# Dealing the rows of tiles 4 to 63 to gather units of falling width, with sums added onto the output

## What is computed

```python
h = jnp.maximum(_layernorm(x, axis=-1), 0.0)
hw = (h @ W.T).reshape(n, 8, 32)
attn = einsum(hw, a_src)[:, None, :] + einsum(hw, a_dst)[None, :, :] + adj[:, :, None] * We[:, 0] + be
attn = jnp.where((adj > 0)[:, :, None], attn, -jnp.inf)
attn = softmax(leaky_relu(attn, 0.2), axis=1)
out = x + einsum('ijh,jhd->ihd', attn, hw).reshape(n, 256) + h @ Wr.T + br
```

## Time and profile before

| | us |
|---|---|
| median of 3 runs | 2900.41 |
| profiled execution, whole time | 2904.47 |
| its span, first to last instruction | 2902.8 |
| front, to the first MAX8 | 0 to 217 |
| gather stage | 217 to 2590 |
| dense stage | 2590 to 2903 |
| VectorE busy | 2346.5 (81%) |
| GpSimd busy | 1844.2 (64%) |
| ScalarE busy | 1625.0 (56%) |
| TensorE busy | 1587.1 (55%) |

### The profile page before, as it was taken

How to read it: one execution, slowest core, us unless ns; L and a number is a source line. 1 busy time by engine, 2 the same in 40 slices (tenths; PEclk the granted TensorE clock), 3 DMA queues, 4 the chain that set the end, 5 groups by cost and what they waited for, 6 DMA issues and landing times.

```text
span 2902.8 us, 31846 instructions
## 1 busy us (share of the span) xinstructions
PE 1587.1 (55%) x5859; PEld 1067.1 (37%) x5860; DVE 2346.5 (81%) x5737; ACT 1625.0 (56%) x6849; POOL 1844.2 (64%) x1914
## 2 busy tenths in 40 slices
PE   6980044332353554456565667566565656445886
PEld 4650043322242433233333334333333433324665
DVE  3449676676786878799999999999999999929993
ACT  2220022222354665577777878777777867565663
POOL 3654777777777777777777777777777776510000
PEclk9995576666675666666666656566666656667998
DMA  3454634444545555566666677767667666437670
GB/s 97 144 187 139 187 93 113 120 124 142 153 134 158 162 166 167 163 176 200 195 196 202 202 212 211 217 196 221 202 214 211 198 210 208 126 130 171 186 175 2
DMA packets 254494, 486.91 MB, mean 168 GB/s; under 512 B 119232, under 2 KB 150464, under 8 KB 252144
## 3 DMA queue, kind: packets, MB, share of 16 engines
q1 hardware_dynamic: 151280, 319.60, 36.1%
q0 software_dynamic: 84752, 148.94, 19.5%
q10 hardware_dynamic: 18288, 16.65, 1.8%
HBM read 549.09 MB, written 25.76 MB: 198 GB/s over the span
## 4 chain that ended last, share of the span: by engine, by line
issue 31%; DMA 27%; POOL 18%; DVE 11%; PE 8%; ACT 2%; POOLq 1%; SPq 0%; DVEq 0%; ACTq 0%; PEldq 0%
DMA gath<-table,offs 25%; POOL gath L413 18%; DVE work L509 3%; DVE work L505 3%; PE banks L933 2%; PE banks L927 2%; ACT gath L795 2%; DMA adj_sb<-in_adj_dram 1%; PE banks L930 1%; PE banks L1014 1%; PE banks L1004 1%; PE banks L956 1%; DVE adj_sb L681 1%; DVE gath L620 0%; POOLq L413 0%
## 5 line engine op out<-in xcount | busy, mean ns | idle before, releaser
L413 POOL DMA_INDIRECT gath<-table,offs x1637 | 1711.7, 1046 | 611.5 <-issue 411.7
L795 ACT ACTIVATE gath<-gath,prob 128x32 f32<-128x32 f32 x6416 | 1366.4, 307 | 110.5 <-DVE prob L608 110.5
L956 PE MATMUL banks<-gath,ident 128*128 128x256 f32 x1670 | 511.6, 479 | 892.5 <-DVE gath L620 892.5
L963 PE MATMUL banks<-gath,ident 128*128 128x256 f32 x1604 | 631.8, 514 | 281.4 <-ACT gath L795 281.1
L956 PEld LDWEIGHTS banks<-gath,ident 128*128 128x128 f32 x1670 | 407.8, 249 | 1013.2 <-DVE gath L620 935.7
L509 DVE FIND_INDEX8 work<-work,adj_sb 128x8 uint32<-128x176 f32 (+30 forms) x833 | 645.5, 798 | 0.7 <-issue 0.6
L505 DVE MAX8 work<-adj_sb 128x8 f32<-128x176 f32 (+30 forms) x833 | 593.4, 789 | 9.9 <-DMA adj_sb<-in_adj_dram 9.9
L963 PEld LDWEIGHTS banks<-gath,ident 128*128 128x128 f32 x1604 | 329.1, 235 | 556.8 <-ACT gath L795 537.8
L790 ACT ACTIVATE prob<-pre 128x176 f32<-128x176 f32 (+23 forms) x63 | 23.7, 376 | 850.5 <-DVE pre L598 849.6
L620 DVE TENSOR_TENSOR gath<-gath,prob 128x1024 f32<-128x1024 f32 (+8 forms) x171 | 240.2, 1457 | 2.1 <-issue 0.2
L587 DVE TENSOR_TENSOR pre<-pre,gath 128x136 f32<-128x136 f32 (+23 forms) x80 | 24.2, 320 | 263.5 <-DMA gath<-table,offs 258.0
(11 more groups left out here) (110 smaller groups left out, 1589.4 us busy)
## 6 DMA issues: line engine op xcount, KB each, us to landing
adj_sb<-in_adj_dram SPq DMA_DIRECT2D x504, 512.0 KB, 3.7
gath<-dst_rows SPq DMA_DIRECT2D x16, 2048.0 KB, 8.8
gath<-table,offs POOLq DMA_INDIRECT x1637
table<-gath POOLq DMA_DIRECT2D x32, 264.0 KB, 2.9
gath<-in_x_dram SPq DMA_DIRECT2D x32, 256.0 KB, 3.0
resid<-gath POOLq DMA_DIRECT2D x32, 256.0 KB, 2.6
work<-table SPq DMA_DIRECT2D x8, 1024.0 KB, 10.8
res_sb<-resid ACTq DMA_DIRECT2D x63, 128.0 KB
```

The costliest lines, as they stand in the source:

```text
L413: pool.indirect_dma_start(gath[:, ph.slot(b, k), :], None, table[:, :], bass.IndirectOffsetOnAxis(ap=offs[:, b, k:k + 1], axis=0), bounds_ ...
L795: last = s.activation(g, g, ACT.Copy, scale=prob[:, k * H + h:k * H + h + 1])
L956: last = m.matmul(ps_sum[:, b, :], ident[:, :], gath[:, ph.slot(b, k), 0:HD], start=False, stop=False)
L963: last = m.matmul(ps_sum[:, b, :], ident[:, :], gath[:, ph.slot(b, k), 0:HD], start=False, stop=(k == K - 1))
```

## The change

- Tiles 1 to 3 stay as they are ("direct"). Tiles 4 to 63 form groups of 4, 8, 8, 8, 8, 8, 8 and 8 tiles. Within a group all rows are ordered by falling edge count, and the first 128 go to the first unit, the next 128 to the second, and so on. A unit's number of slots is set for its place, for example 36, 26, 24, 22, 20, 18, 17, 15 for tiles 8 to 15. All units together have 1137 slots.
- The lists that `find`, `sort_step` and `decode` make go into `stage` as one record a row (row number, 8 source scores, pairs of offset and edge value; 49 to 109 floats). `count` and `place` on VectorE with `ranks` on TensorE (39 products with a 128x128 weight for 8 tiles, 13 for 4; all but one have 21 to 51 columns) work out each row's rank. GpSimd scatters the records to `lists` in DRAM by rank (`deal`, one indirect DMA a tile) and loads them back in unit order (`load_dealt`).
- Finds run up to 13 units ahead of the softmax (`found`); early steps have two or three finds.
- The front writes x + h @ Wr.T + br to `out` too (one more DMA per unit). A unit's sum is added onto the output rows by an indirect DMA with an add (`store`), issued by GpSimd after the gathers of the unit three later. The product with `resid` and ScalarE's copy and DMAs go.
- Normalization by the sum moves from the probabilities to the finished sum (`evacuate`, VectorE, PSUM to `out_sb`, four buffers).
- `prepare` moves to ScalarE: 8 activations over K columns. Its mask goes: an unused slot now has offset 0, a row of `table` with zeros and a score of -1e30, so every gather moves all 128 rows.
- The key arithmetic has one operation less (L523). The ring has 86 slots.
- Adjacency pieces of tiles below 16 are issued without a wait between them; for tiles 16 to 63 the wait stays.
- The clearing of the ring by GpSimd (L388) goes.

```diff
+GROUPS = ((4, (50, 32, 28, 24)),
+          (8, (36, 26, 24, 22, 20, 18, 17, 15)),
...
+          (56, (20, 13, 11, 10, 9, 8, 7, 6)))
+FOUND = (4, 7, 10, 12, 15, 16, 18, 20, 21, 22)
+LEAD = 13
...
+        self.act_slots = K // 2 if K < 18 else 10 if K < 20 or K > 38 else 14 if K < 32 else 16
...
+    found = [FOUND[u] if u < len(FOUND) else min(len(sources), u + LEAD) for u in range(len(units))]
+        group.ranked_at = min(u for u in range(len(units)) if found[u] >= group.listed)
+        group.dealt_after = min(max(group.ranked_at + 1, group.first - 3), group.first - 1)
+        group.loaded_after = min(group.dealt_after + 1, group.first - 1)
...
+                    if n and so.t >= 16:
+                        sp.wait_ge(S[f"adj_in{b}"], 16 * (c // 2 * PIECES + n))
...
+                    pool.dma_start(by_unit(out, u), rt_sb[:, q, :, :]).then_inc(S[f"res_out{q}"], 16)
...
+            def store(un):
+                pool.wait_ge(S["evac"], un.u + 1)
+                lane = turn(un.store_seq)
+                pool.indirect_dma_start(
+                    out[:, :], bass.IndirectOffsetOnAxis(ap=record(un)[:, 0:1].bitcast(U32), axis=0),
+                    out_sb[:, un.u % OUTS, :], None,
+                    bounds_check=N - 1, oob_is_err=False, compute_op=ALU.add).then_inc(lane, 16)
+            def deal(group):
+                pool.wait_ge(S["ranked"], group.g + 1)
+                for i in range(group.n):
+                    lane = turn(group.deal_seq + i)
+                    pool.indirect_dma_start(
+                        lists[group.g][:, :], bass.IndirectOffsetOnAxis(ap=rank[:, group.g % 2, i:i + 1], axis=0),
+                        stage[:, group.g % 2, i * group.W:(i + 1) * group.W], None,
...
+            for un in units:
+                gather(un)
+                if un.u >= LATE:
+                    store(units[un.u - LATE])
+                for group in groups:
+                    if group.dealt_after == un.u:
+                        deal(group)
+                    if group.loaded_after == un.u:
+                        load_dealt(group)
...
+            def place(group):
+                dve.wait_ge(S["rank_ps"], g + 1)
+                v.tensor_tensor(av, sv, pv, ALU.mult).then_inc(S["rank_picked"], 1)
...
+            def evacuate(un):
+                dve.wait_ge(S["tile_sum"], u + 1)
+                dve.wait_ge(S["recip"], u + 1)
+                if u >= OUTS:
+                    landed(dve, units[u - OUTS].store_seq + 1)
...
+                weight(un)
+                if c is not None:
+                    decode(c)
+                if un.u:
+                    evacuate(units[un.u - 1])
+                for group in groups:
+                    if group.ranked_at == un.u:
+                        count(group)
+                        place(group)
...
+                last.then_inc(S["tile_sum"], 1)
+            def ranks(group):
+                pe.wait_ge(S["above_summed"], group.g + 1)
+                m.matmul(ps_above[:, 0:D], ones[:, :], above_sum[:, 0:D], start=True, stop=True)
+                m.matmul(ps_rank[:, 0:n * D], lower[:, :], same[:, 0:n * D], start=True, stop=False)
+                for i in range(n):
+                    m.matmul(rv[:, i, :], ones[:, :], above_sum[:, 0:D], start=False, stop=False)
+                    for j in range(i):
+                        m.matmul(rv[:, i, :], ones[:, :], same[:, j * D:(j + 1) * D], start=False,
+            for un in units:
+                tile_sums(un)
+                for group in groups:
+                    if group.ranked_at == un.u:
+                        ranks(group)
```

648 lines of the change are left out of this document (349 added, 299 removed), and 8 rows, old and new, of tables (GROUPS, S).

## The result

The changed kernel takes **2837.61 us** (median of 4 runs, 2836.38 to 2843.26); the kernel before took 2902.36 beside it. The ratio is 0.9781, 95% interval [0.9762, 0.98]: 2.2% faster, 64.8 us. The forecast was 2788, range 2735 to 2885. The direction and the range hold, but of the 112 us of gain that the sum gave, 50 are missing. The profiled execution has a span of 2835.8 us, 45 more than the 2791 of the sum.

The account below looks back on a forecast made before the run. GpSimd and VectorE were taken to bound late tiles, VectorE alone after the change. Start 208 + 10 + 1888 + 184 = 2290; with 182 + 8, 2480; with 1 + 310, 2791 of span, adjusted to 2788 us; range 2735 to 2885.

Parts of the forecast that it names:

- VectorE's sum: Gather stage: VectorE's removed and added operations net 144 us less, from 2084 us of elapsed work to 1940.
- wait for the first 75 gathers: Before the first softmax: VectorE, done with finds 1 to 3, waits 10 us for gathered rows to land.
- VectorE's work to the last ranking: Gather stage up to the end of the last find's step: 1940 us less 52 in the tail, 1888 us.
- eight waits for ranks: `place` on VectorE waits for ScalarE's slots, then TensorE's rank products, 17 to 33 us a group, 184 us in all.
- tail with the adds: After the last ranks: GpSimd's remaining 118 DMAs, 163 us, and last landings; 182 us plus 8 for the adds.
- adjacency queue: Rival, tiles 16 to 63: SyncE's serial adjacency pieces become the bound at 28.4 us a tile, +40, 2830 us; chance 0.20.
- row at 13.9 us: Profile row of four TensorE records of 16 columns in 0.87 us: upper bound for rank products, 0.22 us a record.
- row at 100.8 us: Profile row used as the lower bound for TensorE's rank products, 0.11 us a record; 0.18 was taken.
- rival of the upper clock: TensorE's ranks run at the upper clock, costing little more than ScalarE's slots: -42, 2745 us; chance 0.15.
- 3.3% put on top for starts: Gather stage: VectorE's 2015.6 us busy divided by 0.967, from 773.4 of 800 us in a late window, 2084 us.
- late adds that stop the lanes: Rival, GpSimd's stores: at a 14 us landing, 2960 us, slower than before; chance 0.13 together with costly descriptors.
- bound by both at once: Late tiles before the change: VectorE's 27.93 us step and GpSimd's 27.6; SyncE's adjacency queue as near, 29.2 us a tile.

Follow-up runs that it names:

- wide units: Changed kernel with each unit as wide as its group's tiles' own maxima, so 1637 slots as before the change: 3406.6 us, ratio 1.1729.
- two edits of the queue: Changed kernel, adjacency pieces of tiles 16 to 63 issued without waits between them: 2783.19 us; or four serial 1 MB pieces in place of eight: 2781.37 us.
- kernel before with free pieces: Kernel before the change, with no wait between the adjacency pieces of any tile: 3018.36 us, ratio 1.04.
- plain store: Changed kernel with the 63 indirect writes of the sums as plain writes, without the add: 2829.32 us (one run).
- experiments on the kernel before: Kernel before the change, adjacency pieces issued without waits between them: 3018.36 us; or in four serial 1 MB pieces: 2968.43 us.

## Why the prediction was right, and where it missed

The direction came from VectorE's sum, and that sum held: 144 us less work forecast, 142 less busy time measured, and the wide units show that the saved slots are what the gain stands on. In time order, forecast and measured:

| step | forecast | measured |
|---|---|---|
| first MAX8 | 208 | 209.4 |
| wait for the first 75 gathers | 10 | 25.4 |
| VectorE's work to the last ranking | 1888 | 1852 |
| eight waits for ranks | 184 | 194.2 |
| waits for adjacency | 0 | 63.2 |
| last ranks placed | 2290 | 2344 |
| tail with the adds | 190 | 178 |
| dense stage | 310 | 313.7 |

(Work: 2344.1, the end of `place` for the last group, less 209.4 and the waits. The dense stage's first load is issued at 2522.1.)

The 45 us by which the span is over the sum are a net figure. The sum was 63 us short on adjacency, 15 on the first gathers, 10 on the ranks, and 5 on the start and the dense stage; it was 36 too high on VectorE's work and 12 on the tail. That these two covered half of the other errors is luck, and only by it do the missing 50 us look like the adjacency queue's 54 alone. The range was wide enough because it had 40 us for the adjacency queue in it.

- **The adjacency queue** is the step that failed. The prediction put it down as a rival at 0.20, 2830 us, for the very reason that the trace then showed: steps of VectorE of 25.3 us beside a chain of 3.67 us a piece. Its own numbers spoke for it: 29.2 us a tile against a forecast step of 25.8. The ones against it (pieces land faster, SyncE catches up in the ranking waits) were only half right: the pieces landed no faster, and the catching up lasts for three finds, after which MAX8 waits again (1697.61). The two edits of the queue give 54 and 56 us. The 29.2 came from 48 waits in a window of 200 us; the queue's real pace in the changed kernel is 28.2, nearer to the rival's own 28.4, and the rival's price of 40 us was a little low.
- **The ranks.** The mechanism held, and each size within 4 us: 16.3, 35.3, 35.4, 22.9, 24.2, 22.3, 20.9 and 16.9 us, for 20, 33, 32, 23, 21, 19, 19 and 17. The part in front of the products is 82 us as forecast (81); the products take 112.6 us for 103, which is nearly all of the 10 us. They did not run at one pace. The products of tiles 32 to 39 stand in TensorE's timeline so (the first and the last two rows):

```profile
1601.92 0.30 PE L1089 MATMUL banks<-above_sum,ones 128*128 128x23 f32 x2
...
1614.94 3.16 PE L1094 MATMUL banks<-work,ones 128*128 128x23 f32 x14
1617.93 0.60 PE L1096 MATMUL banks<-above_sum,ones 128*128 128x23 f32 x2
```

  From 1601.92 to 1618.53 there are 78 records, 0.213 us each: the bound of the row at 13.9 us, not 0.18. The four groups of tiles 8 to 23, 32 to 39 and 40 to 47 run so. The first group does not:

```profile
537.93 0.32 PE L1089 MATMUL banks<-above_sum,ones 128*128 128x51 f32 x2
...
540.67 0.39 PE L1096 MATMUL banks<-above_sum,ones 128*128 128x51 f32 x2
```

  Its 26 records take 3.1 us, 0.114 apart, the bound of the row at 100.8 us. The windows of four groups (the first, tiles 8 to 15, 32 to 39, 56 to 63; the number before the DMA share is the granted clock) show why:

```profile
537.90:541.00 3.10, 3.10 (x27) 3.00 (x26) 0.00 (x0) 0.00 (x0) 2.49 (x3) 1.00 0.43 104
819.80:836.90 17.10, 17.10 (x79) 16.74 (x77) 0.00 (x0) 1.39 (x5) 0.00 (x0) 0.50 0.00 1
1601.90:1618.50 16.60, 16.60 (x79) 16.49 (x77) 0.00 (x0) 1.74 (x7) 0.00 (x0) 0.51 0.47 137
2330.90:2342.90 12.00, 12.00 (x79) 11.97 (x78) 0.00 (x0) 1.49 (x6) 0.00 (x0) 0.71 0.00 0
```

  At 1.00 (2.4 GHz) a record takes 0.114 us, at 0.50 (1.2 GHz) 0.22, and the groups at 0.57 to 0.71 changed level on the way. Ahead of the first group TensorE had worked on sums without a break since 509.74. So the value of 0.18 between the bounds is not one that any record has; it stands for a mix, and the mix here was 0.11 to 0.22 a group. The rival of the upper clock, 42 us cheaper, is out as a whole, though one group and parts of three ran at it.
- The Trainium skill ("TensorE: Matmul & The Clock Gate", section LDWEIGHTS) gives 107 ns for a weight of 128 columns by its formula, an estimate that names no clock. The trace agrees where the granted clock is 1.00 (0.114 us a record, and 0.11 in the row at 100.8 us) and shows twice that where it is 0.50 (0.213). For the front's row at 13.9 us, with 0.22 a record, the profile's clock does not say: its first entry comes at 32 us.
- **First gather wait**: 25.4 for 10. VectorE came to it at 352.9, as forecast (378.34 less 25.41), and the gathers began at 259.2. But up to 380 us GpSimd's gathers waited 22.0 us for landings, and 3.4 before. Here the pieces of the first tiles are issued all at once, and the sum had taken the 8 us that this gives at the start, and not its price. The kernel before with free pieces has that difference alone, and waits 13.4 us, so about 10 of the 19 us are the crowding. The rest isn't shown; that each gather now moves all 128 rows is a candidate. In order: before, before with free pieces, changed kernel, each from 200 to 380 us:

```profile
POOL gath L413 <- DMA gath<-table,offs: 3.4, 11, 0.3
```

```profile
POOL gath L411 <- DMA gath<-table,offs: 13.4, 23, 2.2
```

```profile
POOL arena L490 <- DMA arena<-table,own: 22.0, 16, 2.3
```

- **VectorE's work** came out 36 us lower than summed. The terms held: weighted slots 183.3 us (182 forecast), `evacuate` 419 ns each (0.45), count and place 30 us (27). Busy time from 209.4 to 2344.1 is 1833.5 us, where the sum's terms give 2015.6 - 144 - 52 = 1820. The excess is the 3.3% put on top for starts, 68 us, read from one late window: in the changed kernel what is neither busy nor a listed wait is 18 us, and in the whole gather stage of the kernel before 43.
- **The adds**: 1.63 us of GpSimd and a landing of 4.2, where 2 and 6 were taken. They hide as the prediction said. The rival on the other side, late adds that stop the lanes, would need a landing of 12 us, and the plain store is only 8 us faster. It is refuted.
- **Small records in dealing**: 60 scatters of 196 to 436 B an element land in 2.2 us, sooner than gathers of 1 KB rows (3.5). The Trainium skill ("DMA: Bandwidth & Descriptors", Specifications) has a read-modify-write below 512 B; a landing of one more gather, 4 us, as the prediction worked it out by that page, does not show here. Whether a part of the 2.2 us is such a price no run separates, since none has larger records.
- **The tail** went at GpSimd's pace, 178 for 190 us: 1.5 us for each of its 118 DMAs, all else in it included, where the sum had 1.38 and 27 us around them.

Of the three that the prediction called "bound by both at once" and "as near", the third was no equal. The experiments on the kernel before show that its gathers had no slack, with waits for landings that more adjacency traffic makes longer, and that a shorter adjacency chain gained nothing. It became a bound only when the change took GpSimd's gathers away and made VectorE's step shorter than the chain.

## What to carry to other kernels

When a change takes away the bound, put the next queue's pace beside the new step, not beside the old one: here 29.2 us a tile against 25.8 stood in the prediction itself, was given 0.20, and cost 54 us. Before a wait between transfers is taken away, ask whose landings it protects: the same kind of edit was worth 54 us here (tiles 16 to 63) and cost 113 us in the kernel before (all tiles; some 85 of it after the 16th find). And a wait that is removed gives back only what the next waits behind it leave; a ledger of all waits of the bound engine, run by run, shows where the rest went.

## What the hardware showed

- One DMA piece of 1 MB lands in 5.3 us where one of 512 KB takes 4.0 (medians), so four in a chain move 4 MB in about 21 us from the first issue to the last landing, where eight take 32. Eight pieces issued at once land in 8.6 us each in the median (changed kernel) and make another queue wait for its gathers: from 138 to 349 us in the kernel before.
- An indirect DMA with an add costs GpSimd 1.63 us for 1.02 without, and lands 1.0 us later; a scatter of small records costs 1.00 and lands in 2.2.
- A gather with unused slots takes GpSimd as long as one without (1046 ns and 1034 in the mean), but an offset out of bounds moves nothing: GpSimd's queue moved 148.94 MB in the kernel before, where the 124,159 edges are 131 MB, the front's writes 17, and 128 rows in each of 1637 gathers would be 221. Gathers that all move 128 rows land in 4.1 us when 1637 run, and in 3.5 when 1137 do.
- An fp32 product with a 128x128 weight and 21 to 51 moving columns costs 0.11 us a record (two records each) at a granted clock of 1.00 and 0.21 to 0.22 at 0.50. The same 286 products took 112.6 us behind the sums and 125.8 when TensorE came to them out of an idle stretch.
